# TensorE's loop over the routed blocks of two mixture-of-experts stages written out, with experts' numbers loaded four at a time

## The reference, cut to what matters

```
x = x + attn_a(layernorm(x)); x = x + ffn(layernorm(x))
x = x + attn_b(layernorm(x)); x = x + ffn(layernorm(x))      # x: 16 x 256 x 128

def ffn(x):                                # D=128, I=512, E=8 experts, top 2
    probs = softmax(x @ gate_w + gate_b)
    values, indices = top_k(probs, 2);  values = values / (sum(values) + 1e-9)
    h = gelu(x @ ew1[e] + eb1[e]);  out_e = h @ ew2[e] + eb2[e]
    return x + mlp_shared(x) + sum over the two chosen e of value_e * out_e
```

## Time and profile before

| | |
|---|---|
| median of 3 runs | 931.43 us |
| lowest, highest | 930.83, 938.78 us |
| span of the profiled execution, first to last instruction | 795.6 us |
| stage 0, first up to last routed down | 142.2 to 264.0 us |
| stage 1, first up to last routed down | 637.8 to about 761.6 us |
| mean granted TensorE clock | 0.933 |

### The profile page before, as it was taken

The page is one execution under the profiler, slowest core; times in us unless marked ns, Lnnn a source line. Parts: engine busy times, 40 slices in busy tenths (PEclk is TensorE's granted clock), DMA queues, the critical chain, the costliest instruction groups (busy, mean ns, idle before and its releaser), DMA issues.

```text
span 795.6 us, 22802 instructions
## 1 busy us (share of the span) xinstructions
PE 660.2 (83%) x7807; PEld 475.0 (60%) x7808; DVE 626.3 (79%) x1404; ACT 535.2 (67%) x1288; POOL 481.8 (61%) x504
## 2 busy tenths in 40 slices
PE   0665498899999948989889989989969899999991
PEld 0433488898988933343343444443438779898891
DVE  7799886777777268998997999899855367787838
ACT  3865867666666443887886889878864566666640
POOL 4998601787884378676087736027777637777730
PEclk9999599999999975998996999999998989999996
DMA  7232300233336111010001100000112322322236
GB/s 209 57 103 33 102 7 11 68 92 83 89 82 73 45 44 37 5 35 21 2 2 27 29 2 2 2 2 23 51 54 83 90 64 75 90 80 87 70 113 211
DMA packets 52521, 46.88 MB, mean 59 GB/s; under 512 B 8787, under 2 KB 44795, under 8 KB 52456
## 3 DMA queue, kind: packets, MB, share of 16 engines
q1 hardware_dynamic: 43368, 28.02, 12.5%
q0 software_dynamic: 9088, 17.98, 8.8%
HBM read 26.76 MB, written 20.13 MB: 59 GB/s over the span
## 4 chain that ended last, share of the span: by engine, by line
PE 46%; DVE 25%; ACT 9%; POOL 9%; issue 7%; DMA 2%; SPq 1%; DVEq 0%; ACTq 0%; POOLq 0%
PE ps L932 23%; PE ps L1076 13%; DVE mx L2411 9%; POOL rows L870 7%; PE ps L1333 3%; PE ps L1091 2%; PE ps L1116 2%; DVE xres L2285 2%; ACT xn L1466 2%; ACT scratch L1684 1%; DVE hlo L2404 1%; DVE hhi L2398 1%; PE ps L1346 1%; DVE stats L1786 1%; ACT h L1553 1%
## 5 line engine op out<-in xcount | busy, mean ns | idle before, releaser
L1553 ACT ACTIVATE h<-ps,b1T 128x256 f32<-128x256 f32 x440 | 172.1, 479 | 49.7 <-PE ps L932 46.1
L2411 DVE TENSOR_REDUCE mx<-ps 128x2 f32<-128x512 f32 x256 | 171.3, 683 | 19.5 <-PE ps L932 18.5
L1684 ACT ACTIVATE scratch<-ps 128x512 f32<-128x512 f32 x256 | 152.7, 614 | 38.1 <-PE ps L932 36.8
L932 PE MATMUL ps<-xg,w1s 128*128 128x256 f16 x936 | 116.9, 275 | 12.1 <-issue 9.6
L768 POOL DMA_INDIRECT scratch<-rows,tok_i x78 | 90.4, 1159 | 58.8 <-DVE tok_i L2189 35.3
L1076 PE MATMUL ps<-w2s,hhi 128*128 x1248 | 117.2, 219 | 0.0
L881 POOL DMA_INDIRECT ytok<-yst,didx x78 | 89.4, 1146 | 43.4 <-DVE yst L2219 22.7
L932 PE MATMUL ps<-kst,qst 32*128 32x256 f16 x512 | 99.5, 289 | 17.6 <-DVE mx L2411 14.7
L932 PEld LDWEIGHTS ps<-xg,w1s 128*128 x936 | 87.8, 99 | 26.2 <-issue 16.1
L1579 ACT ACTIVATE xg<-ps 128x512 f16<-128x512 f16 x78 | 46.6, 598 | 79.1 <-PE ps L1116 79.1
L2159 DVE SCALAR_TENSOR_TENSOR hlo<-h,hhi 128x1024 f16<-128x1024 f32 x78 | 95.6, 1226 | 2.7
(11 more groups left out here) (318 smaller groups left out, 1361.4 us busy)
## 6 DMA issues: line engine op xcount, KB each, us to landing
gy<-rows SPq DMA_DIRECT2D x39, 136.0 KB
ysorted<-yst SPq DMA_DIRECT2D x39, 128.0 KB
h<-in_L_ffn_ew SPq DMA_DIRECT2D x16, 256.0 KB, 3.0
scratch<-ytok SPq DMA_DIRECT2D x16, 256.0 KB, 3.4
xres<-in_L_attn_a_x SPq DMA_DIRECT2D x4, 512.0 KB, 5.6
rows<-hl SPq DMA_DIRECT2D x4, 512.0 KB, 3.1
out_x<-xres SPq DMA_DIRECT2D x3, 512.0 KB, 4.5
scratch<-rows,tok_i POOLq DMA_INDIRECT x78
```

Of the source, the lines that this page charges most:

```text
L932: return pe.matmul(o, a, b, start=start, stop=stop)
L1553: last = act.activation(h32[:, u % 2, f], HB[u % 2][:, f], ACT.Gelu_apprx_tanh, bias=b1T[:, ds(e * CH + c, 1)], scale=1.0 / PS)
L1684: act.activation(prb[:, (s // 4 * 4 + (s + 2) % 4) % 8, :], ps[:, s % 2, :], ACT.Exp, scale=HD ** -0.5 / (PS * PS))\
L2411: dve.tensor_reduce(mx[:, c, j:j + 5:4], ps[:, 2 + s % 2, :].rearrange("p (n k) -> p n k", n=2), AX_X, ALU.max).then_inc(Att.mx, 1)
```

## The change

TensorE's loop over the routed blocks is gone: a Python loop writes out all 39 blocks of both stages. Experts' numbers now come in fours at multiples of 4 (0, 4, 8, ... 32, and 3 at 36); each load but the first stands between a turn and a down, in the middle of a block. ScalarE keeps a loop, of 8 iterations instead of 9, moved so that it also loads 4 at 4i; its first four and last three blocks are written out. The work and its order on both engines stay.

```diff
-                es = experts(0, 2)
+                es = list(experts(0, 4))
                 up_routed(0, 0, es[0])
                 turn(2, 2, 0)
                 up_routed(1, 1, es[1])
-                with pe.Fori(0, LOOPED) as i:
-                    es = experts(4 * i, 6)
-                    for u in range(4):
-                        n = 4 * i + u
-                        up_routed(n + 2, (u + 2) % 4, es[u + 2])
-                        turn(n + 3, (u + 3) % 4, i + (u + 3) // 4)
-                        down_routed(n, u, es[u])
-                es = experts(NBLK - 3, 3)
-                for u in range(3):
-                    if u < 1:
-                        up_routed(NBLK - 1, 2, es[2])
+                for n in range(NBLK):
+                    if n + 2 < NBLK:
+                        up_routed(n + 2, (n + 2) % 4, es[(n + 2) % 8])
                     else:
-                        up_shared(m.ahead + u - 1)
-                    down_routed(NBLK - 3 + u, u, es[u])
+                        up_shared(m.ahead + n + 2 - NBLK)
+                    if n + 3 < NBLK:
+                        turn(n + 3, (n + 3) % 4, (n + 3) // 4)
+                        if (n + 3) % 4 == 0:
+                            at = (n + 3) % 8
+                            es[at:at + 4] = experts(n + 3, min(4, NBLK - n - 3))
+                    down_routed(n, n % 4, es[n % 8])
...
-                es = experts(0, 2)
+                es = experts(0, 4)
                 gelu_routed(0, 0, es[0])
-                copy_out(2, 2)
-                gelu_routed(1, 1, es[1])
-                with act.Fori(0, LOOPED) as i:
-                    es = experts(4 * i + 2, 4)
+                for u in range(1, 4):
+                    copy_out(u + 1, (u + 1) % 4)
+                    gelu_routed(u, u, es[u])
+                with act.Fori(1, LOOPED) as i:
+                    es = experts(4 * i, 4)
                     for u in range(4):
                         n = 4 * i + u
-                        copy_out(n + 3, (u + 3) % 4)
-                        gelu_routed(n + 2, u, es[u])
-                gelu_routed(NBLK - 1, 2, experts(NBLK - 1, 1)[0])
+                        copy_out(n + 1, (u + 1) % 4)
+                        gelu_routed(n, u, es[u])
+                es = experts(4 * LOOPED, REST)
+                for u in range(REST):
+                    n = 4 * LOOPED + u
+                    if u + 1 < REST:
+                        copy_out(n + 1, u + 1)
+                    gelu_routed(n, u, es[u])
```

## The result

The change ran in **919.3 us** (median of 4: 916.74 to 929.03) against 931.9 us for the kernel before (median of 4: 930.83 to 938.78): ratio **0.9872 [0.9823, 0.9921]**. The forecast was 921.1 us. The number held, but of the reasoning behind it one assumption was wrong and one holds only on some chips. That came out because the later runs fell on chips of **two kinds**: on some the kernel before takes about 931 us ("slow chips", the kind timed above), on others about 796 us ("quick chips", the kind on which the profile shown of before was taken; its span is 795.6 us). On one quick chip the change took 785.5 us against 797.2 us, ratio 0.9889 [0.9807, 0.997] (run c_after2), on another 786.5 against 795.0 us, 0.989 [0.9856, 0.9924] (run extra_loads).

A forecast was written before the change was run, and what follows sets the result against it. The prediction took TensorE to bound both routed stages, with its loop edges fully on the path. 13.5 us of edges less 1.4, 1.0 and 0.8 us gave 10.3 us, so 931.4 became 921.1 us, range 918.0 to 928.5 us.

The forecast's parts named there:

- The time outside the span: Whole run: 135.8 us between the profiled span of 795.6 us and the runs' median, taken as unchanged.
- Edges removed: TensorE's loop edges in both routed stages: 13.2 us of waits go, plus 0.3 us at stage 0's start.
- The length of a load: TensorE's aligned load of four numbers: 0.31 us in stage 0, 0.41 us in stage 1.
- The rival of long loads: TensorE's loads of four stay long, 0.8 or 1.0 us each: 928.2 or 931.7 us in all; chance 0.17.
- Their exposure: Loads of four before downs, eight in each stage: 0.04 us each in stage 0, 0.14 in stage 1, 1.4 us lost.
- If that cover were gone: Mid-block loads without the 0.53 us of work already handed on, sequencer just behind a wait for rows: up to 0.57 us each.
- The threes: The two loads of three numbers at block 36: 0.78 us long, exposed by 0.51 us each, 1.0 us lost.
- Late rows: Stage 1's turns waiting for rows when code packets meet row transfers: 0.8 us lost, bounds 0 and 3.9; stage 0 nothing.
- rows arrive late in stage 1: Rival: 13 packets at 0.45 us each delay stage 1's rows, 5.9 us instead of 0.8, 926.2 us; chance 0.13.
- Code packets: TensorE's written-out code: 26 more packets, some 68 in all, the fetch itself costing nothing; rival of stalls 947.1 us, chance 0.05.
- Sum: Whole kernel: 13.5 - 1.4 - 1.0 - 0.8 = 10.3 us gained.

The follow-up runs named there:

- c_after2: The change, unedited, run again on a quick chip: 785.5 us against 797.2 us for the kernel before, ratio 0.9889.
- extra_loads: The change plus unused loads of three numbers, which were not in the program that ran, so the change itself; quick chip: 786.5 us against 795.0 us before.
- c_before: The kernel before, unedited, run again and profiled on a slow chip: 934.9 us, ratio 1.0085.
- unroll_oldloads: Against the change: TensorE written out, but six numbers loaded before every fourth up, ScalarE as before; quick chip: 791.1 us, ratio to before 0.9932.
- loop_fours: The kernel before with its loops, but TensorE loads four aligned numbers at the loop's top and two in mid-block; quick chip: 791.5 us, ratio 0.995.
- two_products: The change without the third product of the routed downs (16 matmuls, not 24); quick chip: 779.1 us, ratio to before 0.983.
- c_after: The change, unedited, run again on a slow chip: 931.8 us against 933.3 us before, ratio 1.0051.

## Why the prediction was right, and where it was not

*The time outside the span: wrong.* I took 135.8 us between the profiled span and the runs' median as an outer part. It doesn't exist: the change's own span is 915.2 us at 917.05 us, c_before's 938.2 at 940.0, so 1.8 us lie outside. The shown profile was of a quicker execution than the timed ones, by all signs on another chip. So the sum was worked out for one kind of chip and set against the other's time. By the quick chips' own times it reads 795.0 - 10.3 = 784.7 and 797.2 - 10.3 = 786.9, and 786.5 and 785.5 us were measured.

*Edges removed, 13.2 + 0.3 us: right on quick chips.* All 6.2, 5.8 and 1.2 us went, and at stage 0's start 1.9 us of waits for an up became 1.1 us (0.8 us for the 0.3). unroll_oldloads and loop_fours show the reason that I gave, branch and load on one lead, from both sides. On slow chips an edge lies beside a copy that is late anyway; its 0.69 us buy far less there.

*The length of a load: right.* 0.31 and 0.41 us forecast, 0.333 and 0.332 us measured; the 0.10 us that I added in stage 1 for its slower six was not needed. The rival of long loads falls, with its 0.8 and 1.0 us. So does the floor of about 600 ns that the Trainium skill, "DMA: Bandwidth & Descriptors" (Latency and other measured facts), gives: 0.308 us for one number and 0.333 us for four lie at half of it.

*Their exposure, 1.4 us: right in size, wrong in kind.* I spread it over all 16. In c_after2 five of them show, each behind a turn that came late, with 0.36 to 0.49 us (2.1 us; 1.3 us in three in extra_loads, one of these behind a turn on time); the others show nothing. "If that cover were gone each would cost up to 0.57 us" was the true case.

*The threes, 1.0 us.* 0.81 and 0.77 us long, exposed by 0.71 and 0.15 us in c_after2 (0.56 and 0.15 in extra_loads).

*Late rows, 0.8 us: the term that was mis-sized.* Matmul starts give 3.8 us more of it than in the trace of before (c_after2: 2.95 in stage 0, 0.86 in stage 1) and 3.7 us (extra_loads: 1.7 and 2.0). In stage 1 the mechanism is the one that I gave, a code packet in the time of a row transfer: 0.86 and 2.0 us for my 0.8, inside the bounds of 0 and 3.9 us. The rest of the miss is stage 0, where I charged nothing, since GpSimd was to need 2.5 us a block. That came from its shortest gather, 0.96 us. The mean over 160:240 of the same trace is another:

```profile
L768 POOL DMA_INDIRECT scratch<-rows,tok_i x54 | 64.8, 1199 | 16.5 <-issue 13.7 <-PE ps L1116 2.7
```

54 gathers of 1.20 us and 16.5 us between them fill the 80 us: 3.0 us for the two of a block. 2.7 us of the time between them were waits for TensorE, and some of the long gathers may have been held back too; without TensorE in its way two_products shows 2.85 us. Against 2.87 us that is no slack. The rival "rows arrive late in stage 1" (5.9 us in place of 0.8) has the right mechanism and too high a price: it charged 0.45 us for each of 13 packets, and only 2 to 4 of a stage's packets made a turn late.

*Code packets: right.* 67 packets; 11 of them in 160:250, where the loop had none, and no gap that only a packet explains (none at 202.6, 209.8, 216.8 or 225.5). What they cost is late rows in stage 1.

*Sum, from the parts for c_after2:* -13.2 - 0.8 + 2.1 + 0.9 + 3.8 = -7.2 us, against 7.0 us by the stage windows; for extra_loads -13.2 - 0.7 + 1.3 + 0.7 + 3.7 = -8.2 and 8.0. The forecast was -10.3; the 2 to 3 us between are the late rows. The medians gave 11.7 us (c_after2) and 8.5 us, both with intervals that hold 7 to 8 us.

*The 12.6 us of the first measurement* are more than the 3 to 8 us that the slow traces show in the routed stages. Its interval, 7.4 to 16.5 us of 931.9, doesn't overlap with c_after's, -13.6 to +4.2 us gained, on a chip of the same kind. But that is with three executions of before left out; with all seven the gain of c_after is 0.7 us with an interval of about -8 to +10 us (my estimate from the single times), and the two overlap. So I can't say whether anything differs between the chips or loads of the program, or whether both are noise. That the forecast hit 919.3 within 2 us is in the main luck: the sum belongs to quick chips, where 7 to 8 us were gained, and the time that it was taken from to slow chips, where the removal of the edges shows as 1.4 us in stage 0.

## What to carry to other kernels

Set a profile's span against its own execution's time before a sum is made: here 1.8 us lay outside, and a "part outside" of 135.8 us meant that profile and timings were of different chips. Before two medians are compared, look at the granted clock of the single executions: here it made 6.5 us for one and the same kernel on one chip. A load of registers or a branch was free here as long as the engine's sequencer led: count both against one lead (here 0.70 us), align fours, and put loads where the lead is rebuilt. Take a neighbour's period from the mean of its instructions over the stage, not from a short one: small regular gaps are what keeps it ahead.

## What the runs showed of the hardware that was not expected

- The same kernel takes 795 to 797 us on two chips and 931 to 933 us on slow chips. In attention the granted clock is 0.95 and 0.84. In the routed blocks it is 1.00 in both, but ScalarE's copy of a turn starts 0.88 us after the last matmul's end in place of 0.04 us (medians, 156 to 250 us). What delays the report isn't known.
- A TENSOR_LOAD of one number takes 0.308 us and of an aligned four 0.333 us on TensorE; two and three take 0.55 and 0.78 us, so each number outside an aligned four adds 0.235 us. ScalarE's four took 1.02 us from 4i + 2 on the earlier trace rows and 0.31 us from 4i on.
- The end of a loop of some 400 instructions took 0.57 us of TensorE's lead although no packet was fetched in it; the step out of the loop costs as much as a back edge.
- A code packet (16 KB, about 1 us on one DMA engine) that started 2.0 to 2.95 us before a turn of stage 1 went with a late turn in 21 of 31 cases, by 0.08 to 1.15 us; none of the 249 other turns looked at was late.
